# Layer 0's ramp in another order, and 28 instead of 32 row maxima ahead of the exponentials, in a fused cross-attention and expert kernel on one Trainium2 core

## The reference

```
x   : (4, 512, 256)        ctx : (4, 512, 256)        16 heads of 16
Q = heads(layernorm(x) @ Wq)   K = heads(ctx @ Wk)   V = heads(ctx @ Wv)
scores = einsum('bhqd,bhkd->bhqk', Q, K) / 4
attn   = softmax(scores, axis=-1)
out    = einsum('bhqk,bhkd->bhqd', attn, V)
x = x + tanh(g[0]) * (out @ Wo)
x = x + tanh(g[1]) * ffn(layernorm(x))
```

## Time and profile before

| | |
|---|---|
| timed runs | 928.46, 928.73, 932.31 us; median 928.73 |
| the profiled execution's own time | 923.2 us |
| its span in the profile | 921.6 us |
| busy: PE / DVE / ACT / POOL | 849.6 / 630.0 / 498.9 / 162.4 us |
| mean granted PE clock | 0.974 |
| layer 0: first maximum / first score for an exponential | 52.9 / 76.5 us |
| layer 1: first score for an exponential | 529.8 us |

### The profile page before, as it was taken

One profiled execution on the slowest core, in us unless ns is written; L12 is line 12 of the kernel. 1 busy time (PEld: TensorE's weight loads), 2 busy tenths in 40 slices (PEclk: granted clock), 3 DMA queues, 4 the chain that ended last, 5 costly groups with the idle time before them and its releaser, 6 DMA issues.

```text
span 921.6 us, 14451 instructions
## 1 busy us (share of the span) xinstructions
PE 849.6 (92%) x4544; PEld 474.4 (51%) x4545; DVE 630.0 (68%) x1242; ACT 498.9 (54%) x663; POOL 162.4 (18%) x285
## 2 busy tenths in 40 slices
PE   8789999999997999999996899999999979993398
PEld 6442333333357999999964333333334644441387
DVE  5889888888773222224258988888886578688942
ACT  1536777777752222222234577777777683587660
POOL 1223011111147000000054333000005313000000
PEclk9999999999999999999998999999999999997699
DMA  9595846656346111111169864343410000000011
GB/s 276 157 242 139 216 118 168 166 164 172 124 152 224 36 34 34 34 34 38 40 208 252 209 179 84 82 83 81 81 42 2 1 1 1 0 0 0 1 41 51
DMA packets 71328, 91.40 MB, mean 99 GB/s; under 512 B 26087, under 2 KB 56935, under 8 KB 71271
## 3 DMA queue, kind: packets, MB, share of 16 engines
q1 hardware_dynamic: 63564, 67.96, 29.3%
q0 software_dynamic: 5584, 19.93, 6.4%
q10 hardware_dynamic: 2128, 2.89, 1.0%
HBM read 62.90 MB, written 27.44 MB: 98 GB/s over the span
## 4 chain that ended last, share of the span: by engine, by line
PE 76%; DVE 11%; DMA 4%; issue 3%; ACT 3%; POOL 2%; SPq 1%; DVEq 0%; ACTq 0%
PE PS L1867 13%; PE PS L1835 13%; PE PS L1856 11%; PE PS L2025 9%; PE PS L2010 8%; PE PS L2091 8%; PE PS L2112 5%; PE PS L1966 3%; DVE MX L1363 2%; POOL BIG L705 2%; PE PS L1881 1%; PE PS L1798 1%; DVE cmx L1663 1%; DVE BIG L1660 1%; DMA X<-in_x 1%
## 5 line engine op out<-in xcount | busy, mean ns | idle before, releaser
L1363 DVE TENSOR_REDUCE MX<-PS 128x1 f32<-128x512 f32 x512 | 320.7, 682 | 43.4 <-PE PS L1835 42.8
L974 ACT ACTIVATE Pt<-PS 128x1024 f32<-128x1024 f32 x256 | 248.3, 1021 | 102.6 <-PE PS L1856 102.6
L1835 PE MATMUL PS<-KSt,BIG 96*128 96x512 bf16 x512 | 175.2, 386 | 10.5 <-DVE MX L1363 3.7
L1856 PE MATMUL PS<-BIG,KSt 99*128 99x512 bf16 x512 | 151.0, 381 | 0.2 <-DMA BIG<-MR 0.2
L1867 PE MATMUL PS<-Pt,VS 128*17 128x512 f32 x1024 | 136.1, 598 | 0.0
L1835 PEld LDWEIGHTS PS<-KSt,BIG 96*128 96x128 bf16 x512 | 40.5, 97 | 155.3 <-DVE MX L1363 98.0
L2010 PE MATMUL PS<-KSt,Pt 128*128 128x128 f32 x736 | 86.0, 275 | 1.3 <-issue 1.3
L2010 PEld LDWEIGHTS PS<-KSt,Pt 128*128 128x128 f32 x736 | 85.6, 192 | 2.6 <-issue 1.4
L1492 DVE COPY KSt<-PS 128x256 f32<-128x256 f32 x23 | 9.8, 425 | 112.0 <-PE PS L1997 112.0
L2091 PE MATMUL PS<-KSt,BIG 128*128 128x512 f32 x192 | 83.2, 593 | 1.6 <-DVE KSt L1586 0.9
L1856 PEld LDWEIGHTS PS<-BIG,KSt 99*128 99x128 bf16 x512 | 49.9, 98 | 53.2 <-ACT Pt L974 2.4
(11 more groups left out here) (199 smaller groups left out, 1081.9 us busy)
## 6 DMA issues: line engine op xcount, KB each, us to landing
qk_parts<-BIG SPq DMA_DIRECT2D x64, 192.0 KB, 3.2
BIG<-in_w POOLq DMA_DIRECT2D x12, 1024.0 KB, 5.8
BIG<-qk_parts SPq DMA_DIRECT2D x32, 192.0 KB, 3.3
KSt<-qk_parts SPq DMA_DIRECT2D x32, 192.0 KB, 3.8
v_rows<-BIG SPq DMA_DIRECT2D x8, 544.0 KB, 5.2
VS<-v_rows SPq DMA_DIRECT2D x32, 136.0 KB, 3.0
BIG<-qk_parts SPq DMA_DIRECT2D x32, 128.0 KB, 3.9
KSt<-qk_parts SPq DMA_DIRECT2D x32, 128.0 KB, 4.0
```

What stands on the lines that cost most here:

```text
L974: act.activation(PP[:, 2 * (kc % 2) + half, :, :].rearrange("p h t -> p (h t)"), ST[half], ACT.Exp, scale=DK ** -0.5).then_inc(exp_done, 1)
L1363: dve.tensor_reduce(MX[:, g % 2, i % TB, i // TB:i // TB + 1], ring(i), AX.X, ALU.max, negate=True).then_inc(max_taken, 1)
L1835: pe.matmul(ring(i), QS[0:ROWS, g, h, qc * P:(qc + 1) * P], KS[0:ROWS, g, h, :], start=True, stop=True).then_inc(max_done, 1)
L1856: last = pe.matmul(ST[half][:, i * S:(i + 1) * S], KS[0:ROWS + PARTS, g, h, kc * P:(kc + 1) * P], QS[0:ROWS + PARTS, g, h, :], start=True, ...
```

## The change

It has two parts.

1. *Both layers:* `LEAD = 4`. A step now makes the last 4 maxima of the next group in its round 0, and the first 12 of the group beyond in rounds 1 to 3. The ramp makes 16 + 12 = 28 maxima instead of 32, and step 14 of a layer, which made none, makes the last 4 of step 15. `turn_max` moves in round 1 from behind the second to behind the fourth maximum, and into bank 7; in step 14 `turn_tile` for tile 0 moves behind the four maxima.
2. *Layer 0's ramp in another order on all five engines:* `x` is normalised in two pieces (tiles 0 to 7 and 8 to 15); the value halves are copied by ACT (`take_half`) instead of DVE, all through bank 6 and into one buffer per batch (`VBS`); keys 3 and the turn of `x` 3 stand ahead of the first maximum, the last values behind it; layer 0's queries use banks 2 and 3 too; SP stores and loads in another order. Layer 1's ramp keeps its order, but for `turn_max`, which stands two maxima and one projection step earlier.

```diff
+        VBS = BIG[...]  (one VB for each batch)
-        TURNED_MAX = RING[0]
+        TURNED_MAX = RING[2]
+        LEAD = 4
+        def step_place(i):
+            return (i + LEAD) % 16
         def ring(i):
-            return RING[(i + (i >= 6) + (i >= 12)) % 3]
+            j = step_place(i)
+            return RING[(j + (j >= 8) + (j >= 12)) % 3]
...
-        NORMS = [("first0", range(TB)), ("first1", range(TB, 2 * TB)), ("first2", range(2 * TB, NT)), ...
+        NORMS = [("first0", range(2 * TB)), ("first1", range(2 * TB, NT)), ...
...
 # SP
+            def prep_first():
+                store_parts(0, "k", 0); store_values(0, 0)
+                sp.wait_ge(ones_kept, 16); load_ones()
+                store_parts(0, "k", 1)
+                sp.wait_ge(v_out, 16)
+                for g in range(NG):
+                    load_v(0, 0, g)
+                store_parts(0, "q", 0); store_values(0, 1)
+                ... (waits until q 0 has landed)
+                load_stack(0, 0, 0); store_parts(0, "k", 2); load_stack(0, 0, 1)
+                store_parts(0, "q", 1); load_stack(0, 0, 2)
+                store_parts(0, "k", 3); load_stack(0, 0, 3)
+                store_values(0, 2); store_parts(0, "q", 2)
+                store_parts(0, "q", 3); store_values(0, 3)
...
 # ACT
+            def take_half(p, half):
+                act.wait_ge(v_done, 2 * p + half + 1)
+                act.activation(value_rows(0, p)[...], value_bank(0, half)..., ACT.Copy).then_inc(v_taken, 1)
+            def prep_first():
+                act.wait_ge(ab_in, AB_IN[0])
+                high_part(0, "k", 0, 0)
+                take_half(0, 0)
+                middle_part(0, "k", 0, 0); high_part(0, "k", 0, 1)
+                norm("first0")
+                middle_part(0, "k", 0, 1); take_half(0, 1)
+                high_part(0, "k", 1, 0); high_part(0, "k", 1, 1)
+                copy_xnt(0, 0)
+                middle_part(0, "k", 1, 0); middle_part(0, "k", 1, 1)
+                high_part(0, "q", 0, 0); high_part(0, "q", 0, 1)
+                copy_xnt(0, 1)
+                middle_part(0, "q", 0, 0); middle_part(0, "q", 0, 1)
+                take_half(1, 0)
+                norm("first1")
+                ...
 # DVE
             def prep_first():
-                rests(0, "k", 0)
-                link(dve, norm_rstd("first0"))
-                norm_writes("first0", 0, 0, NORM_TILES["first0"])
-                take_values(0, 0)
...
+                rest_of(0, "k", 0, 0)
+                norm_var("first0")
+                rest_of(0, "k", 0, 1)
+                link(dve, norm_rstd("first0"))
+                route_ranks()
+                norm_writes("first0", 0, 0, NORM_TILES["first0"])
+                rests(0, "k", 1)
+                link(dve, norm_stats(NORM_TILES["first1"], "first1"))
+                norm_var("first1")
+                rests(0, "q", 0)
+                link(dve, norm_rstd("first1"))
+                norm_writes("first1", 0, 2, NORM_TILES["first1"][:TB])
+                rests(0, "k", 2)
+                norm_writes("first1", 0, 3, NORM_TILES["first1"][TB:])
+                rests(0, "q", 1)
+                maxima(0, 0, range(2))
+                ...
+                maxima(0, 1, range(8))
+                dve.wait_ge(v_taken, 2 * B)
+                dve.memset(PV, 0.0).then_inc(pv_zero, 1)
+                maxima(0, 1, range(8, 16 - LEAD))
...
 # DVE, in a step
+                        if not (last and g == NG - 1):
+                            maxima(n + (g + 1) // NG, (g + 1) % NG, range(16 - LEAD, 16))
                         if early and not layer:
                             (last_group_2, last_group_3)[g - 2](n)
                             continue
                         if ahead:
-                            maxima(n + (g + 2) // NG, (g + 2) % NG, range(12))
+                            maxima(n + (g + 2) // NG, (g + 2) % NG, range(8))
...
 # PE, in a round
-                                if early and i == 2:
+                                if early and i == 2 and (g > 2 or kc > 0):
                                     turn_tile(layer, TB * (g - 2) + kc, 4)
...
+                                if kc == 0 and not (last and g == NG - 1):
+                                    max_scores(n + (g + 1) // NG, (g + 1) % NG, range(16 - LEAD + i, 17 - LEAD + i))
+                                elif kc > 0 and not early:
+                                    max_scores(n + (g + 2) // NG, (g + 2) % NG,
+                                               range(4 * kc - LEAD + i, 4 * kc - LEAD + i + 1), ...)
+                                if early and g == 2 and kc == 0 and i == 3:
+                                    turn_tile(layer, 0, 4)
-                                if kc == 1 and i == 1 and not (last and g == NG - 1):
+                                if kc == 1 and i == 3 and not (last and g == NG - 1):
                                     turn_max(...)
```

More of the change, by code:

```diff
@@ new lines, in prep_second @@
+            def prep_second():
+                store_parts(1, "k", 0)
+                store_values(1, 0)
+                store_parts(1, "k", 1)
+                store_values(1, 1)
+                store_parts(1, "q", 0)
+                store_parts(1, "k", 2)
+                store_values(1, 2)
+                for c in range(KC):
+                    sp.wait_ge(part_out[slot("q", 0, c)], landed(1, "q", 1))
+                load_stack(1, 0, 0)
+                load_stack(1, 0, 1)
+                store_parts(1, "q", 1)
+                store_values(1, 3)
+                load_stack(1, 0, 2)
+                store_parts(1, "k", 3)
+                load_ones()
+                load_stack(1, 0, 3)
+                sp.wait_ge(v_out, 16 * (B + 1))
+                sp.wait_ge(tr_done, KC * (B + 2))
+                load_v(1, 0, 0)
+                load_v(1, 0, 1)
+                store_parts(1, "q", 2)
+                load_v(1, 0, 2)
+                load_v(1, 0, 3)
+                store_parts(1, "q", 3)
+                load_quantised()
@@ L1771, in key_step @@
             def key_step(layer, p, c, kc):
-                if kc == 0 and p > 0:
+                if kc == 0 and not layer:
+                    wait(pe, r_done, made(0, "k", p, c) - 1)
+                elif kc == 0 and p > 0:
                     pe.wait_ge(r_done, made(layer, "k", p - 1, c) + 1)
-                elif kc == 0 and layer:
+                elif kc == 0:
                     pe.wait_ge(gelu_done, 2 * SLOT_TILES - 2)
-                mm = pe.matmul(qk_bank("k", p, c), weight(layer, 1)[:, kc, c * P:(c + 1) * P],
+                mm = pe.matmul(qk_bank(layer, "k", p, c), weight(layer, 1)[:, kc, c * P:(c + 1) * P],
                                context(layer, p)[:, kc, :], start=(kc == 0), stop=(kc == KC - 1))
@@ L1788, in project_step @@
             def project_step(layer, p, c, kc):
-                if kc == 0 and p == 0 and layer:
+                if kc == 0 and not layer:
+                    pe.wait_ge(r_done, made(0, "q", p, c) - 1)
+                elif kc == 0 and p == 0:
                     pe.wait_ge(ys_ready, SLOT_TILES)
@@ L1807, in project_queries, with value_steps @@
                         project_step(layer, p, c, kc)
-            def project_values(layer, p):
+            def value_steps(layer, p, some):
                 n = B * layer + p
-                for t in range(TB):
-                    if p > 0:
+                for t in some:
+                    if not layer:
+                        if t % 2 == 0:
+                            wait(pe, v_taken, 2 * n + t // 2)
+                    elif p > 0:
                         pe.wait_ge(v_taken, 2 * (n - 1) + t // 2 + 1)
-                    elif layer:
+                    else:
                         pe.wait_ge(xst_ready, SLOT_TILES)
                     for kc in range(KC):
-                        last = pe.matmul(bank(6 + t // 2)[:, (t % 2) * D:(t % 2) * D + D],
+                        last = pe.matmul(value_bank(layer, t // 2)[:, (t % 2) * D:(t % 2) * D + D],
                                          context(layer, p)[:, kc, t * P:(t + 1) * P],
@@ L1875, in turn_outputs @@
                 if ahead is not None:
[L1876 removed]
+                    pe.wait_ge(max_taken, 16 * ahead + 6)
                 else:
```

487 lines of the change are left out of this document (287 added, 200 removed).

## The result

The changed kernel takes 939.64 us (median of 4 runs, 937.87 to 942.5) against 928.67 us of the kernel before in the same runs: ratio 1.0109, 95% interval 1.0089 to 1.013: 10 us slower by the ratio, 11 by the medians. The forecast was 929.6 with a range up to 935.5, so the time lies outside it. Two executions that took more than twice the usual time (3018 us in experiment 3, 2202 us of the kernel before beside experiments 5 to 8) are in none of the ratios.

A forecast was written before the change was run, and what follows sets the result against it. PE was taken to bound the kernel, with DVE near its limit where maxima mix with projections. Layer 0's +0.1 and layer 1's +0.8 gave +0.9, making 929.6 us on the timed median, range 924 to 935.5.

The forecast's parts named there:

- The ordinary steps: Both layers' attention steps: maxima and reductions unchanged, the later hop still covered, so 11.93 us as before, 0 change.
- Step 14 and the end: End of each layer: four maxima cost PE 1.1 us, wait for DVE 1.0 more; +2.0 per layer, bounds 1.1 and 2.5.
- The tile's wait: Step 14, ahead of the first `turn_tile`: PE idles 1.4 us until DVE has taken the last maximum, 1.0 more than before.
- The transfers: Late transfer of turned maxima: +0.5 at layer 0's step 2 with the fill, +0.4 at layer 1's step 1.
- Layer 0's ramp: Start to first score: first maximum at 50.3, first score at 74.1 instead of 76.47; -2.4 us, bounds -5 and about 0.
- The walk: Layer 0's ramp followed engine by engine up to the first maximum at 50.3, past ACT's square root by 34.9.
- the sum itself: Layer 0, first maximum to first score: PE's 17.1 us plus 2.4 lost give 69.8; five maxima and the memset, 74.1.
- my list of what would prove me wrong: Waits in batches 1 and 2, turn waiting for POOL, clock falling elsewhere in ramp, first maximum over 3 us off 50.3.
- Layer 1's ramp: With four maxima fewer ahead, the first score starts at 528.2 instead of 529.81: -1.6 us, bounds -2.5 and -0.5.
- The second: Rival: layer 0's ramp pays 5.8, each end costs 1.1, no late hop; -5.2, 923.5 us; chance 0.13.
- The third: Rival: eight layer 0 steps with weight loads wait 1.2 us each for the hop; 9.6 more, 939 us; chance 0.17.
- the sum's +0.9: Whole kernel: layer 0 +0.1 and layer 1 +0.8, taking the profiled execution from 923.2 to 924.1 us.

The follow-up runs named there:

- experiment 3: Kernel before with only layer 0's new ramp, LEAD = 0; ratio 0.9934 to the kernel before.
- experiments 5 to 8: New ramp, LEAD = 2, 0.997; LEAD = 4 alone, 1.0149; new ramp, LEAD = 0, three idle matmuls per maximum, 0.9979; changed kernel with moved fill, 1.0095.
- Experiment 1: Kernel before with the turn of the maxima behind the fourth maximum of round 1, bank 7, LEAD = 0; ratio 1.0069.
- 9: Kernel before with the turn of the maxima moved from ahead of to right behind the values of round 1; ratio 0.9991.
- experiment 8: Changed kernel with the 3 MB fill of zeros moved from step 1 to layer 0's last step; ratio 1.0095 to the kernel before.
- experiment 6: Kernel before with the LEAD = 4 edits in both layers, layer 0's ramp in its old order; ratio 1.0149.
- experiment 11: New ramp, LEAD = 2, copy first in layer 1's ramp, one idle matmul per late ramp maximum in layer 0; 922.58 us, ratio 0.9916 to the kernel before.
- 4: Changed kernel with the first output tile's turn moved behind the scores of the next round; ratio 1.0086 to the kernel before.
- 2: Changed kernel with ACT's copy of the turned maxima ahead of queries 3's high part in layer 1's ramp; ratio 1.0055 to the kernel before.

## Why the prediction was wrong

- **The ordinary steps, the step that failed.** "The maxima and their reductions are the same in number and place; I take 11.93 us as before." The maxima are, but the turn is not, and I priced only whether POOL would be in time for it. It costs 0.41 us between maxima and scores instead of the 0.18 in its old place (experiments 1 and 9): 0.23 in a step, and over steps 1 to 13 of both layers 5.7 us measured.
- **Step 14 and the end.** +2.9 each instead of +2.0. The tile's wait was about as worked out (1.26 against 1.4). Missing was the wait behind the later turn: ACT's tile copy stands behind the copy of the maxima, and PE waits 0.96 for it. Experiment 1, without a late maximum, has 0.97 of it and is 1.4 longer at each end; so the turn's place makes 1.4 of the 2.9 and the four maxima 1.5.
- **The transfers.** At step 2 +1.3 beside the step's own 0.2, not +0.5, and +3 where the clock falls behind the wait. In layer 1's step 1 no wait of the kind for which +0.4 was put. By the Trainium skill's rule ("DMA: Bandwidth & Descriptors", the section Queues, rings and completion order) it would have been 0; the 7.0 us here and experiment 8, where only the fill moved, speak against it as the earlier trace rows did.
- **Layer 0's ramp.** Better than said: first maximum 48.8 for 50.3, first score 71.87 for 74.1. The walk held up to the square root (34.8 to 35.0 for 34.9). The column operations behind it then took 1.9 us instead of 2.9, and PE from the turn of `x` 2 to the first maximum 10.4 instead of 11.0. In the stretch behind, the sum itself was off: 69.8, five maxima and the memset make 73.4, not 74.1, and PE lost 1.1 up to the turn where 2.4 were put. But my list of what would prove me wrong had the clock falling elsewhere in the ramp, and it did, from 71 to 78, behind PE's waits for DVE, and step 0 lost 2.0. In experiment 6, LEAD = 4 with the old ramp, the clock stayed up in step 0, and from the first score to the turn were 4.90 us instead of 7.57.
- **Layer 1's ramp.** -1.3 for -1.6 up to the first score, but not for the reason given. The base, 529.81, came from a ramp with a fall of the clock (granted 0.93 in the earlier trace rows) that the sum took as the ramp's own length. Without a fall the old ramp takes 23.76 us and the new one 24.11: four maxima fewer, and it is no shorter, because I had not read ACT's order around the moved turn. With the copy ahead it takes 22.7 (experiment 11, LEAD = 2). The +2.1 in step 0 is the clock's longer fall: from the first score to the turn are 8.41 us in the changed kernel and 6.13 in experiment 8, where it stayed up. It fell in the changed kernel and in experiments 4 and 6 and not in 8, with the same waits of PE in the ramps of all four.
- **The rivals.** The second, a ramp that pays by 5.8 and cheap ends, had its ramp (71.9 for 70.7, and 0.9934 when alone, though the profile shows only 2.5 us of that) but not its ends. The third had the size (939) by a mechanism that isn't there: no step with a weight load waited for its transfer in the changed kernel, and the lengthening is the same in both layers. Slower was right, its reason wrong.

Against the sum's +0.9 the stretches add up to about 10 more: the turn in steps 1 to 13 5.7, both steps 0 and their slower clock 4.1, the ends 1.8, the transfers 0.4, less 1.9 for two ramps that looked better than forecast.

What stays open: how much of the difference between 4, 8 and the changed kernel is real, since the intervals overlap (that of 2, up to 1.0087, ends just below the changed kernel's 1.0089); and what decides whether the clock falls in layer 1's step 0, since PE's 1.25 us alone does not, as 8 shows.

## What to carry to other kernels

Price a moved instruction by its neighbours at both places: the same narrow matmuls cost half as much beside other narrow ones as between wide ones, and a quarter of a microsecond in each step outweighs a ramp. Then list, on each engine that serves it, what stands behind the operation in program order, since the copy of something else may be what comes late. Move only as far as the place holds: two late maxima left the step as it was, four didn't. And before one profile is taken as the base of a sum, or two are set against each other, look at the granted clock of each stretch: here a fall of 1.4 us hid what a better order gained, and another one passed for a gain that wasn't there.

## What the runs showed of the hardware

A turn of 12 columns adds 0.18 to 0.20 us next to the 17-column matmuls of the values and 0.41 between 128-column ones. PE's clock fell to 1.2 GHz for some 3 to 7 us in layer 0's new ramp, where PE kept waiting for DVE (granted 0.61 and 0.79 over 8 us), and one idle matmul of 0.22 us behind each 0.22 us maximum kept it up (1.00). In layer 1 it fell in some profiles and not in others with the same waits (0.60 and 1.00 over the same 8.44 us). A 12 KB transfer took 7.0 us behind a 3 MB fill from another queue and made no wait once the fill was elsewhere.
